# Values of two steps dealt together, three buffers of probabilities, one pair of lows less, head shares and epsilon on GpSimd

## The chip, the core and the metric

The kernel runs on one core of a Trainium2 chip, as one launch. The metric is the time of the launch on the device in microseconds, as the median of several runs. The engines are named as in the profile: PE is TensorE, with PEld its weight loads, DVE is VectorE, ACT is ScalarE, POOL is GpSimd, SP is SyncE, which here only issues DMAs.

## What is computed

Eight batches of 512 tokens with 256 features go through four blocks one after the other. They hold six attentions of 16 heads with 16 features a head: in block 0 a self-attention with a window of 64 and a linear bias and a cross-attention to the context, in block 1 a causal self-attention and a cross-attention (both with folded projections), in block 2 a cross-attention of normalized inputs, in block 3 a last cross-attention. Blocks 0 to 2 also have a feed-forward of 1024 features. The core of the reference is, for each attention:

```python
q = (qx @ wq + bq).reshape(Bq, Lq, H, DH).transpose(0, 2, 1, 3)
k = (kx @ wk + bk).reshape(Bq, Lk, H, DH).transpose(0, 2, 1, 3)
v = (kx @ wv + bv).reshape(Bq, Lk, H, DH).transpose(0, 2, 1, 3)
s = jnp.einsum('bhqd,bhkd->bhqk', q, k) / jnp.sqrt(DH)    # + bias, masked
a = jax.nn.softmax(s, axis=-1)
o = jnp.einsum('bhqk,bhkd->bhqd', a, v).transpose(0, 2, 1, 3).reshape(Bq, Lq, D)
x = _layernorm(x + o @ wo + bo, g, b)                      # then gelu(x @ w1 + b1) @ w2 + b2
```

## The kernel before

The work is 48 loops: for each pair of batches the six attentions, and within one attention the even batch and then the odd one (`LOOPS`). A loop (b, a) has 16 steps: 4 groups of 4 heads, each over 4 tiles of 128 keys. Its kinds of work, called stages, are these:

- `scores` b, a, n, e (L890, with L893 or L895 for masks): for step n, keys on the partitions and up to 512 queries in the columns, in two halves e of two heads (one half where the columns are few). They fill one of two PSUM pairs `st`. ACT takes the exponential of a pair into `probs` (L1066), which has two buffers of 4 x 512 columns.
- `values` b, a, n (L915): four heads side by side in groups of 32 columns of TensorE, probabilities in fp32 moving, accumulated over the 4 key tiles into `pv`. A step shows as 8 records of 128*32. PE waits for the exponentials of the step; the exponential of step n waits until the values of step n-2 are done.
- `sums` (L1075): ACT copies `pv` of a group into `sums`. `heads` (L1163 to L1184): DVE transposes it into `turned`, takes the reciprocal of the denominators (`rec`), multiplies (`normal`, the "shares", L1176), and for every second group transposes `normal` into `oT`.
- `low` b, "o", p: `oT` is split into a high part `oh` by ACT (L1034) and a low part `ol` by POOL (L1276). The same stages split the layer's input x into `xh`, `xl` and the context into `ch`, `cl`. They are fp32r operands of the products of L564.
- `max` (L867): for a later loop's or a later group's heads PE computes the scores once more with bf16 operands, one matmul of up to 512 columns for 128 queries, into one of three PSUM banks `mx`; DVE reduces each to the row maximum (L1149, or L1152 with a mask). POOL masks the queries for it (`qm`, L1259), up to four heads ahead (`RING`). The same three banks take the projections, the output product, and `rows` and `add`.
- `rows`, `stats`, `scale`, `turn`: output product and residual, layer norm, and the transposition back. In `stats` DVE computes mean and variance, adds epsilon (`spread_of`, L1214), and POOL raises it to the power -0.5 (`rstd`, L1287).

Every engine runs the stages in one common order, `PLAN`, each taking its own part of a stage and waiting on semaphores for the others' parts. `PLAN` is dealt from up to six streams: 0 the steps of this loop (`step_stages`), 1 the maxima of this loop, 2 "between", which is the tail of the loop before and the start of the next one, 3 the context's part of the next loop, 4 the weights, 5 the folding at the start. `MERGE` holds for each kind of loop a string of digits: the stream from which the next stage is taken. In stream 0 the values of step n-1 stand behind the scores of step n. The first `low` of an attention's output stands in stream 0 in group 2, the second in the tail.

## Time and profile before

| | us |
|---|---|
| median of 3 runs | 3447.16 |
| lowest and highest | 3444.5, 3450.5 |
| the profiled execution | 3444.64 |
| its span, first to last instruction | 3442.4 |
| PE busy | 3285.2 |
| DVE busy | 2632.1 |
| ACT busy | 2181.7 |
| POOL busy | 1701.0 |

The span is one execution of the program. A busy time is the union of an engine's instructions; matmuls overlap in the pipeline and their ends are modelled, so that short stalls of PE vanish in its busy time, and only starts tell them. The mean granted clock of TensorE is 0.994 of full speed. The chain of work that ended last is spread over many lines: 67% of the span on PE and 22% on DVE. POOL and DVE work at the same time most of the time.

### The profile page before, as it was taken

How to read it: one execution, taken by the hardware profiler on the slowest of the kernel's cores; microseconds unless marked ns; L12 is line 12 of the kernel's file. 1: busy time of each engine (PE TensorE's matmuls, PEld its weight loads, DVE VectorE, ACT ScalarE, POOL GpSimd, SP SyncE). 2: the span in 40 equal slices, each digit the busy share in tenths (PEclk: the TensorE clock that was granted, in tenths of full speed). 3: DMA queues.
4: the chain of work that ended last, by engine and by line, in shares of the span. 5: the costliest groups of instructions: out<-in, count | busy, mean ns of one | idle time of the engine just before them, and what ended most of it. 6: DMA issues, size and time to landing. Idle time of an engine off the chain costs nothing.

```text
span 3442.4 us, 57665 instructions
## 1 busy us (share of the span) xinstructions
PE 3285.2 (95%) x20149; PEld 1782.5 (52%) x20436; DVE 2632.1 (76%) x6523; ACT 2181.7 (63%) x2831; POOL 1701.0 (49%) x1497
## 2 busy tenths in 40 slices
PE   7999999999999999999999999999999999999998
PEld 5556545544555655554454565554446456455443
DVE  4976887766897697866789669776689966977667
ACT  3565766666666666666656656666575666766665
POOL 6634654444663464444475345344457435533443
PEclk9999999999999999999999999999999999999999
DMA  7322421223321232122343132122234322212211
GB/s 220 122 63 69 132 73 63 87 68 106 117 94 53 92 116 66 62 84 69 114 128 99 53 103 89 59 66 84 75 123 127 103 66 87 88 49 74 75 62 56
DMA packets 304449, 304.23 MB, mean 88 GB/s; under 512 B 52050, under 2 KB 278226, under 8 KB 302226
## 3 DMA queue, kind: packets, MB, share of 16 engines
q1 hardware_dynamic: 278436, 298.18, 27.2%
q10 hardware_dynamic: 25728, 2.36, 0.6%
q8 instruction: 165, 2.70, 0.3%
q14 instruction: 120, 0.98, 0.1%
HBM read 217.60 MB, written 82.84 MB: 87 GB/s over the span
## 4 chain that ended last, share of the span: by engine, by line
PE 67%; DVE 22%; issue 3%; ACT 3%; POOL 2%; DMA 1%; SPq 1%; POOLq 0%; another core or an unknown queue 0%; ACTq 0%; DVEq 0%
PE pv L915 12%; DVE row_max L1149 11%; PE st L890 11%; PE mx L867 10%; PE mx L564 10%; PE st L564 10%; PE mx L971 6%; PE mx L949 3%; DVE mx L1152 2%; DVE y L1220 2%; PE mx L967 2%; ACT probs L1066 2%; DVE normal L1176 1%; DVE turned L1172 1%; PE st L986 1%
## 5 line engine op out<-in xcount | busy, mean ns | idle before, releaser
L1066 ACT ACTIVATE probs<-st 128x1024 f32<-128x1024 f32 (+1 forms) x1344 | 1271.6, 976 | 693.0 <-PE st L890 435.6
L1149 DVE TENSOR_REDUCE row_max<-mx 128x1 bf16<-128x512 f32 x2048 | 1296.6, 683 | 217.2 <-PE mx L867 167.6
L1259 POOL TENSOR_TENSOR qm<-q_high,own_rows 128x512 bf16<-128x512 bf16 x768 | 794.7, 1047 | 463.1 <-PE mx L867 424.4
L867 PE MATMUL mx<-k_high,qm 128*128 128x512 bf16 (+3 forms) x2785 | 816.3, 343 | 64.0 <-DVE row_max L1152 25.0
L890 PE MATMUL st<-q_packed,k_packed 97*128 97x512 bf16 (+2 forms) x3072 | 804.8, 345 | 32.0 <-ACT probs L1066 15.1
L915 PE MATMUL pv<-probs,va 128*32 128x512 f32 (+2 forms) x6144 | 703.9, 532 | 10.7 <-ACT probs L1066 3.7
L867 PEld LDWEIGHTS mx<-k_high,qm 128*128 128x128 bf16 x3072 | 267.3, 97 | 685.4 <-DVE row_max L1149 220.6
L890 PEld LDWEIGHTS st<-q_packed,k_packed 97*128 97x128 bf16 (+1 forms) x3072 | 279.3, 98 | 357.6 <-ACT probs L1066 111.4
L1152 DVE CUSTOM_DVE_ANT_0 mx<-mx,tab 128x192 f32<-128x192 f32 (+4 forms) x1024 | 399.8, 441 | 80.4 <-PE mx L867 63.2
L1287 POOL TENSOR_TENSOR rstd<-spread_of,m_half 128x2 f32<-128x2 f32 x144 | 99.9, 694 | 484.9 <-DVE spread_of L1214 484.4
L915 PEld LDWEIGHTS pv<-probs,va 128*32 128x32 f32 x6144 | 124.9, 108 | 243.6 <-issue 196.5
L1195 DVE TENSOR_TENSOR y<-mx,row 128x256 f32<-128x256 f32 x224 | 92.5, 421 | 201.6 <-PE mx L971 173.3
L971 PE MATMUL mx<-w2s,hid 128*128 128x256 f32 x1024 | 231.6, 379 | 0.0
L1276 POOL TENSOR_TENSOR ol<-oT,oh 128x512 fp32r<-128x512 f32 x96 | 122.4, 1275 | 217.4 <-ACT oh L1034 217.4
L1276 POOL TENSOR_TENSOR xl<-xT,xh 128x512 fp32r<-128x512 f32 x116 | 148.6, 1282 | 156.9 <-ACT xh L1034 156.6
L1081 ACT ACTIVATE hid<-st,col 128x512 f32<-128x512 f32 x192 | 121.6, 685 | 130.6 <-PE st L564 130.1
L971 PEld LDWEIGHTS mx<-w2s,hid 128*128 128x128 f32 x1024 | 189.5, 190 | 23.1
L1265 POOL TENSOR_TENSOR sq<-raw_w,sq 128x512 fp32r<-128x512 f32 x93 | 119.5, 1285 | 143.0 <-ACT sq L1016 143.0
L564 PE MATMUL st<-xh,w1s 128*128 128x512 f32 x384 | 162.3, 423 | 0.0
L1075 ACT ACTIVATE sums<-pv 128x512 f32<-128x512 f32 x192 | 114.8, 598 | 67.2 <-PE pv L915 59.0
L564 PE MATMUL st<-xh,w1l 128*128 128x512 f32 x384 | 151.7, 395 | 0.0
L1220 DVE TENSOR_SCALAR y<-y,moments,rstd 128x256 f32<-128x256 f32 x288 | 145.8, 548 | 5.0 <-POOL rstd L1287 4.9
(119 smaller groups left out, 4752.9 us busy)
## 6 DMA issues: line engine op xcount, KB each, us to landing
k_packed<-k_parts_dram SPq DMA_DIRECT2D x576, 128.0 KB, 2.7
q_packed<-q_parts_dram SPq DMA_DIRECT2D x576, 128.0 KB, 2.7
q_parts_dram<-q_low SPq DMA_DIRECT2D x96, 256.0 KB, 2.1
k_parts_dram<-k_low SPq DMA_DIRECT2D x96, 256.0 KB, 2.2
raw_w<-squares_dram SPq DMA_DIRECT2D x69, 256.0 KB, 3.0
q_parts_dram<-q_high SPq DMA_DIRECT2D x48, 256.0 KB, 2.1
k_parts_dram<-k_high SPq DMA_DIRECT2D x48, 256.0 KB, 2.1
raw_w<-w_dram SPq DMA_DIRECT2D x48, 256.0 KB, 2.9
```

What stands on the lines that cost most here:

```text
L564: mm = pe.matmul(bank, stationary.bitcast(F32R), moving.bitcast(F32R), start=start and n == 0, stop=stop and n == len(parts) - 1)
L867: mm = pe.matmul(bank[:, 0:k1 - k0], qm[:, h % RING, i * P:(i + 1) * P], high["k"][s][:, t, k0:k1], start=True, stop=True)
L890: mm = pe.matmul(flat[:, c:c + w], kk[:, k * P:(k + 1) * P], qq[:, q0:q1], start=True, stop=(k_kind == FULL))
L915: mm = pe.matmul(pv[j * PAIR:(j + 1) * PAIR, q0:q1], va[s][:, k, at:at + PAIR], probs[:, step % 2, c:c + q1 - q0], start=(k == 0 and k_kin ...
L971: mm = pe.matmul(bank[:, 0:D], hid[:, j, at], w2s[:, j, :], start=False, stop=(j == FT - 1))
L1066: act.activation(dst[:, :, 0:w], held["scores", b, a, n, e][:, :, 0:w], ACT.Exp, scale=ATT_SCALE[a]) \
L1081: ins = act.activation(hid[:, n], held["hid", b, f, c][:, e], FFN_ACT[f], bias=cv(f"b1_{f}")[:, n:n + 1])
L1149: ins = dve.tensor_reduce(top, scores, AX_X, ALU.max, negate=True)
L1152: ins = dve.tensor_tensor_reduce(scores, scores, hide[:, hide.shape[1] - (k1 - k0):hide.shape[1]], -1.0, 1e30, ALU.add, ALU.min, top)
L1220: ins = dve.tensor_scalar(y[:, i, :], y[:, i, :], moments[:, i, 0:1], rstd[:, i:i + 1], ALU.subtract, ALU.mult)
L1259: pool.tensor_tensor(qm[:, h % RING], high["q"][s][:, h // HT], own_rows[:, h % HT:h % HT + 1].to_broadcast([P, TOK]), ALU.mult) \
L1276: pool.tensor_tensor(rests[:, k, at].bitcast(F32R), raw(b, tag)[:, k, at], highs[:, k, at], ALU.subtract) \
```

## The change

It does six things. (1) `step_stages` yields the values of two steps, n-2 and n-1, behind the scores of every even step n, and the last two at the end. (2) `probs` has three buffers (`RING_P`), and the exponential of step n waits for the values of step n-3. (3) `oh` and `ol` are gone: the attention output uses `xh` and `xl`, the first `low` of it moves from the steps to the tail, and attention 4's two lows follow both of its additions. `low_reads` makes ACT wait for the last reader of x before it writes them. (4) The shares are made by POOL, and DVE waits for them before it transposes `normal` into `oT` and before the next group's transpose into `turned`. (5) POOL adds epsilon before it raises to the power. (6) All strings of `MERGE` are new; they have the same digits of each kind in another order, save for the stages that moved between streams. Of the strings the diff below shows the first lines of two.

```diff
--- before.py
+++ after.py
@@ -25,6 +25,7 @@
 AHEAD = GRP + 2
 BLK = 32
 RING = 4
+RING_P = 3
 STEPS = NG * TT
 VCOL = HD + 1
 VROW = H * VCOL + HD - 1
@@ -213,12 +214,12 @@
             yield "scores", b, a, n, e
         if k == 2 and g:
             yield "heads", b, a, g - 1
-            if g == 2:
-                yield "low", b, f"o{a}", 0
-        if n:
+        if n and n % 2 == 0:
+            yield "values", b, a, n - 2
             yield "values", b, a, n - 1
             if k == 0:
                 yield "sums", b, a, g - 1
+    yield "values", b, a, STEPS - 2
     yield "values", b, a, STEPS - 1
     yield "sums", b, a, NG - 1
 
@@ -228,7 +229,10 @@
     if tag in TAG_COL:
         for t in range(KT):
             yield "add", b, tag, t
-            if tag in SPLIT_TAGS:
+            if tag in SPLIT_TAGS and tag != "a4":
+                yield "low", b, tag, t
+        if tag == "a4":
+            for t in range(KT):
                 yield "low", b, tag, t
         return
     yield "rows", b, tag, 0
@@ -251,6 +255,7 @@
 
 def tail_stages(b, a):
 
+    yield "low", b, f"o{a}", 0
     yield "heads", b, a, NG - 1
     yield "low", b, f"o{a}", 1
     for tag in AFTER[a]:
@@ -331,36 +336,36 @@
 
 
 MERGE = {
-    "first": "111111141121151101111511125011241012510111011011001515101151120001105110251000101120110112425022"
...
-    "51": "110011011201102000110413111210301112110113400111011100011011412011010030212111010121301041010140"
...
+    "first": "111115145151141145010115511511101051112120110110415101112241510011101041150514105210121012510110"
...
+    "51": "100101110110114013111400211110110110211100100200140114210131001100111421011120301310100113300012"
...
 }
 
 
@@ -404,16 +409,14 @@
         elif kind == "hidden":
             last[low_place(b, FFN_INPUT[stage[2]])] = "st", ("hid", b, *stage[2:])
         elif kind == "add" and stage[2] == "a4":
-            last["o"] = "mx", stage
+            last["x"] = "mx", stage
         elif kind == "rows" and stage[2][0] == "a":
-            last["o"] = "mx", stage
+            last["x"] = "mx", stage
     return before_low
 
 
 def low_place(b, tag):
 
-    if tag[0] == "o":
-        return "o"
     return "c" if tag[0] == "c" or tag == "in" and prefetched(b, 0) else "x"
 
 
@@ -489,13 +492,11 @@
 
         ncT = sb("ncT", [P, KT, TOK])
         oT = sb("oT", [P, KT, TOK])
-        oh = sb("oh", [P, KT, TOK])
-        ol = sb("ol", [P, KT, TOK])
         xh = sb("xh", [P, KT, TOK])
         xl = sb("xl", [P, KT, TOK])
         ch = sb("ch", [P, KT, TOK])
         cl = sb("cl", [P, KT, TOK])
-        lows = {"o": (oh, ol), "x": (xh, xl), "c": (ch, cl)}
+        lows = {"x": (xh, xl), "c": (ch, cl)}
         turned = sb("turned", [P, TOK])
         normal = sb("normal", [P, TOK])
         y = sb("y", [P, TT, D])
@@ -505,7 +506,7 @@
         in_dram = {"q": q_dram, "k": k_dram}
         qm = sb("qm", [P, RING, TOK], BF16)
         max_rows = sb("max_rows", [P, NG, BLK], BF16)
-        probs = sb("probs", [P, 2, GRP * TOK])
+        probs = sb("probs", [P, RING_P, GRP * TOK])
         sums = sb("sums", [P, 2, TOK])
         hid = sb("hid", [P, FT, TOK])
         x_next = [hid[:, s * KT:(s + 1) * KT] for s in range(SLOTS)]
@@ -913,7 +914,7 @@
                         c = column(k_kind, k, j)
                         at = place(g * GRP + j) * VCOL
                         mm = pe.matmul(pv[j * PAIR:(j + 1) * PAIR, q0:q1], va[s][:, k, at:at + PAIR],
-                                       probs[:, step % 2, c:c + q1 - q0],
+                                       probs[:, step % RING_P, c:c + q1 - q0],
                                        start=(k == 0 and k_kind != WINDOW), stop=(k == TT - 1))
                     mm.then_inc(*step_done.mark(("values", b, a, n)))
                 elif kind == "hidden":
@@ -937,7 +938,7 @@
                     bank = held["add", b, "a4", t] = mx_bank()
                     at = slice(t * P, (t + 1) * P)
                     product(pe, bank, [(weight("o", w)[:, j, at], x[:, j, :]) for j in range(KT)
-                                       for w, x in ((0, oh), (1, oh), (0, ol))], True, True) \
+                                       for w, x in ((0, xh), (1, xh), (0, xl))], True, True) \
                         .then_inc(*mx_filled.mark(("add", b, "a4", t)))
                 elif kind == "add":
                     tag, t = stage[2:]
@@ -974,7 +975,7 @@
                             pe.wait_ge(*pool_step.past(("split", b // SLOTS * SLOTS, int(tag[1]), "o")))
                             pe.wait_ge(*pool_step.past(("low", b, f"o{tag[1]}", 1)))
                         mm = product(pe, bank[:, 0:D], [(x[:, j, at], weight("o", w)[:, j, :]) for j in range(KT)
-                                                        for x, w in ((oh, 0), (oh, 1), (ol, 0))], False, True)
+                                                        for x, w in ((xh, 0), (xh, 1), (xl, 0))], False, True)
                     mm.then_inc(*mx_filled.mark(("rows", b, tag, i)))
                 elif kind == "turn":
                     tag, half = stage[2:]
@@ -1058,11 +1059,11 @@
                     q0, q1 = span(k_kind, k)
                     w = (q1 - q0) * len(heads) // 2
                     step = LOOP_NO[b, a] * STEPS + n
-                    if step >= 2:
-                        act.wait_ge(*step_done.nth(step - 1))
                     act.wait_ge(*st_filled.past(("scores", b, a, n, e)))
+                    if step >= RING_P:
+                        act.wait_ge(*step_done.nth(step - RING_P + 1))
                     c = column(k_kind, k, heads[0])
-                    dst = probs[:, step % 2, c:c + 2 * TOK].rearrange("p (b n) -> p b n", b=2)
+                    dst = probs[:, step % RING_P, c:c + 2 * TOK].rearrange("p (b n) -> p b n", b=2)
                     act.activation(dst[:, :, 0:w], held["scores", b, a, n, e][:, :, 0:w], ACT.Exp, scale=ATT_SCALE[a]) \
                         .then_inc(*st_drained.mark(("probs", b, a, n, e)))
                 elif kind == "sums":
@@ -1165,22 +1166,16 @@
                     t, odd = divmod(g, 2)
                     old = (b, a, g - 1) if g else (*before(b, a), NG - 1) if LOOP_NO[b, a] else None
                     blocks = turned[:].rearrange("p (n c) -> p n c", c=BLK)
-                    shares = normal[:].rearrange("p (n c) -> p n c", c=BLK)[:, :, odd * HD:(odd + 1) * HD]
                     dve.wait_ge(*sums_kept.past(("sums", b, a, g)))
                     if old:
-                        dve.wait_ge(*row_step.past(("shares", *old)))
+                        dve.wait_ge(*pool_step.past(("shares", *old)))
                     chain(dve.transpose(turned[:], sums[:, g % 2]), ("turned", b, a, g))
-                    chain(dve.reciprocal(rec[:], blocks[:, :, HD]), ("rec", b, a, g))
-                    if old and not odd:
-                        dve.wait_ge(*row_step.past(("oT", old[0], old[1], old[2] // 2)))
-                    share = dve.tensor_tensor(shares, blocks[:, :, 0:HD],
-                                              rec[:].unsqueeze(2).to_broadcast([P, TOK // BLK, HD]), ALU.mult)
-                    share.then_inc(*row_step.mark(("shares", b, a, g)))
+                    dve.reciprocal(rec[:], blocks[:, :, HD]).then_inc(*row_step.mark(("rec", b, a, g)))
                     if odd:
                         if LOOP_NO[b, a] and not t:
                             pb, pa = before(b, a)
                             dve.wait_ge(*mx_filled.past(("add", pb, "a4", KT - 1) if pa == 4 else ("rows", pb, f"a{pa}", TT - 1)))
-                        dve.wait_ge(*row_step.past(("shares", b, a, g)))
+                        dve.wait_ge(*pool_step.past(("shares", b, a, g)))
                         dve.transpose(oT[:, t], normal[:]).then_inc(*row_step.mark(("oT", b, a, t)))
                 elif kind == "rows":
                     tag, i = stage[2:]
@@ -1210,9 +1205,7 @@
                     chain(ins, ("stats", b, tag, half))
                     for i in (2 * half, 2 * half + 1):
                         ins = dve.bn_aggr(moments[:, i, :], st6[:, i, :])
-                    chain(ins, ("moments", b, tag, half))
-                    dve.tensor_scalar(spread_of[:, at], moments[:, at, 1], EPS, None, ALU.add) \
-                        .then_inc(*row_step.mark(("eps", b, tag, half)))
+                    ins.then_inc(*row_step.mark(("moments", b, tag, half)))
                 elif kind == "scale":
                     tag, half = stage[2:]
                     dve.wait_ge(*pool_step.past(("rstd", b, tag, half)))
@@ -1280,10 +1273,24 @@
                     pool.wait_ge(*act_step.past(("m", b, a, m)))
                     pool.tensor_tensor(low[m][:, 1], rest[m][:], low[m][:, 0], ALU.subtract) \
                         .then_inc(*pool_step.mark(("l", b, a, m)))
+                elif kind == "heads":
+                    a, g = stage[2:]
+                    t, odd = divmod(g, 2)
+                    old = (b, a, t - 1) if t else (*before(b, a), NG // 2 - 1) if LOOP_NO[b, a] else None
+                    blocks = turned[:].rearrange("p (n c) -> p n c", c=BLK)
+                    shares = normal[:].rearrange("p (n c) -> p n c", c=BLK)[:, :, odd * HD:(odd + 1) * HD]
+                    pool.wait_ge(*row_step.past(("rec", b, a, g)))
+                    if old and not odd:
+                        pool.wait_ge(*row_step.past(("oT", *old)))
+                    pool.tensor_tensor(shares, blocks[:, :, 0:HD], rec[:].unsqueeze(2).to_broadcast([P, TOK // BLK, HD]), ALU.mult) \
+                        .then_inc(*pool_step.mark(("shares", b, a, g)))
                 elif kind == "stats":
                     tag, half = stage[2:]
                     at = slice(2 * half, 2 * half + 2)
-                    pool.wait_ge(*row_step.past(("eps", b, tag, half)))
+                    pool.wait_ge(*row_step.past(("moments", b, tag, half)))
+                    pool.tensor_scalar(spread_of[:, at], moments[:, at, 1], EPS, None, ALU.add) \
+                        .then_inc(*pool_step.mark(("eps", b, tag, half)))
+                    pool.wait_ge(*pool_step.past(("eps", b, tag, half)))
                     pool.tensor_tensor(rstd[:, at], spread_of[:, at], m_half[:, at], ALU.pow) \
                         .then_inc(*pool_step.mark(("rstd", b, tag, half)))
                 elif kind == "out" and b + 1 < B:
```

## Rows read from the trace of the kernel before

**Rows 1.** The page: busy us, share of the span and instructions of each engine.

```profile
PE 3285.2 (95%) x20149; PEld 1782.5 (52%) x20436; DVE 2632.1 (76%) x6523; ACT 2181.7 (63%) x2831; POOL 1701.0 (49%) x1497
```

**Rows 2.** Busy us by stretch: sum over six DVE loops, then over six PE loops.

```profile
sum 324.40, PE 309.04 PEld 162.09 DVE 296.44 ACT 216.89 POOL 199.54; mean PE 51.51 PEld 27.01 DVE 49.41 ACT 36.15 POOL 33.26
...
sum 519.90, PE 503.36 PEld 276.85 DVE 359.71 ACT 328.43 POOL 224.19; mean PE 83.89 PEld 46.14 DVE 59.95 ACT 54.74 POOL 37.37
```

**Rows 3.** PE in order of time: start, duration, engine, line, what, count.

```profile
1510.84 0.60 PE L890 MATMUL st<-q_packed,k_packed 97*128 97x512 bf16 x2
1511.28 0.38 PE L867 MATMUL mx<-k_high,qm 128*128 128x512 bf16 x1
...
1515.86 0.59 PE L867 MATMUL mx<-k_high,qm 128*128 128x512 bf16 x2 [0.16 <-issue]
1516.39 1.06 PE L915 MATMUL pv<-probs,va 128*32 128x512 f32 x8
1517.39 0.39 PE L867 MATMUL mx<-k_high,qm 128*128 128x512 bf16 x1
```

**Rows 4.** PE in order of time: a joined pair of steps, and one step alone.

```profile
425.42 0.86 PE L915 MATMUL pv<-probs,va 128*32 128x256 f32 x16
426.21 0.61 PE L867 MATMUL mx<-k_high,qm 128*128 128x512 bf16 x2
...
405.67 0.64 PE L915 MATMUL pv<-probs,va 128*32 128x256 f32 x8
406.25 0.23 PE L867 MATMUL mx<-k_high,qm 128*128 128x128 bf16 x1
```

**Rows 5.** All engines in order of time: the last score step.

```profile
3419.18 1.04 PE L890 MATMUL st<-q_packed,k_packed 97*128 97x512 bf16 x4
...
3419.88 1.94 ACT L1066 ACTIVATE probs<-st 128x1024 f32<-128x1024 f32 x2 [0.32 <-PE st L890]
...
3421.88 1.06 PE L915 MATMUL pv<-probs,va 128*32 128x512 f32 x8 [0.66 <-ACT probs L1066]
```

**Rows 6.** Groups by line and shape: count, busy, mean ns, idle before.

```profile
L1066 ACT ACTIVATE probs<-st 128x1024 f32<-128x1024 f32 x1120 | 1107.0, 1022 | 540.1 <-PE st L890 435.6 <-PE st L893 59.1 <-DVE max_rows L1161 8.9
```

**Rows 7.** Waits: who waited for whom, us in total, times, longest.

```profile
PEld mx L867 <- POOL qm L1259: 28.6, 40, 0.8
...
ACT probs L1066 <- PE pv L915: 13.2, 10, 2.6
```

**Rows 8.** Line 1176 (ns min, median, max), and its busy time in six DVE loops.

```profile
L1176 DVE TENSOR_TENSOR normal<-turned,rec x192: 424/426/2384, 66.7 to 3424.7; 128x256 f32<-128x256 f32 x192
...
sum 324.40, DVE 17.26; mean DVE 2.88
```

**Rows 9.** Groups by line and shape, on DVE.

```profile
L1214 DVE TENSOR_SCALAR spread_of<-moments 128x2 f32<-128x2 f32 x144 | 25.4, 176 | 4.9
```

**Rows 10.** Groups by line and shape, on POOL.

```profile
L1259 POOL TENSOR_TENSOR qm<-q_high,own_rows 128x512 bf16<-128x512 bf16 x768 | 794.7, 1047 | 463.1 <-PE mx L867 424.4 <-ACT q_high L1001 19.4 <-remote 18.5
L1276 POOL TENSOR_TENSOR ol<-oT,oh 128x512 fp32r<-128x512 f32 x96 | 122.4, 1275 | 217.4 <-ACT oh L1034 217.4
...
L1287 POOL TENSOR_TENSOR rstd<-spread_of,m_half 128x2 f32<-128x2 f32 x144 | 99.9, 694 | 484.9 <-DVE spread_of L1214 484.4
```

**Rows 11.** In order of time: the last epsilon and its power.

```profile
3436.24 0.17 DVE L1214 TENSOR_SCALAR spread_of<-moments 128x2 f32<-128x2 f32 x1
...
3436.49 1.06 POOL L1287 TENSOR_TENSOR rstd<-spread_of,m_half 128x2 f32<-128x2 f32 x1 [2.66 <-DVE spread_of L1214]
```

**Rows 12.** In order of time: DVE and POOL around one multiplication of shares.

```profile
969.38 2.15 POOL L1281 TENSOR_TENSOR k_low<-k_rest,k_low 128x1024 bf16<-128x1024 f32 x1
969.42 2.38 DVE L1176 TENSOR_TENSOR normal<-turned,rec 128x256 f32<-128x256 f32 x1
```

**Rows 13.** In order of time: from the last reciprocal to the last transpose.

```profile
3424.38 0.25 DVE L1173 RECIPROCAL rec<-turned 128x16 f32<-128x16 f32 x1
...
3425.13 0.71 DVE L1184 STREAM_TRANSPOSE oT<-normal 128x512 f32<-128x512 f32 x1
```

56 lines of the change are left out of this document (28 added, 28 removed).

## The prediction

> **What bounds the kernel now.** I read the page's busy shares first, then tables by stretch, and only then single instructions. The shares say PE 95% and DVE 76% of the span [rows 1]. Both are too full for an average to tell which one sets the time where, so I cut the span at the last values step of each loop. A group of twelve loops (two batches by six attentions) takes 844 us and recurs four times; I read the second, 897.2 to 1741.5 us. Its loops fall into two classes. In six of them, 324.4 us together, DVE is busy 296.44 us, 91%; in the other six, 519.9 us, PE is busy 503.36 us, 97%, and DVE only 359.71 us, 69% [rows 2]. I call them the DVE loops (attention 0 of both batches, 1 and 3 of the even batch, 2 and 5 of the odd one) and the PE loops. A microsecond saved on PE counts in the PE loops; one saved on DVE counts in the DVE loops; ACT and GpSimd are the fullest engine in neither.
>
> Next I looked at what "busy" PE does around a values step. Eight records of 128*32 are one step. Two ordinary matmuls of 512 columns lie 0.44 us apart from start to start over the pair (1510.84 to 1511.28), 0.22 each. Two that start at 1515.86 should therefore end their streaming at 1516.30; the values step starts at 1516.39, 0.09 late, and the matmul behind it starts 1.00 after it (1517.39) [rows 3]. What part of that 1.00 belongs to entering and leaving the 32-column form is seen where two steps stand together. A pair of 256 and 128 columns takes 0.79 us to the next matmul (425.42 to 426.21); alone, 256 columns take 0.58 (405.67 to 406.25) [rows 4]. From 512 to 256 columns is 0.42 less, so 128 alone should take 0.21 less again, 0.37, and the two alone 0.95. So a step that joins another saves 0.15 or 0.16 inside and 0.09 in front: 0.24 us.
>
> **Part 1: values side by side, -31 us.** Expanding the two order lists (8566 stages each, 5895 of them with matmuls, the same work) and keeping what PE runs, the 768 values steps form 751 blocks before and 517 after. Only 251 of the 384 pairs really stand together; in the rest, most often two or three maxima stand between, so such a pair still enters and leaves twice. Blocks in the PE loops go from 380 to 252: 128 x 0.24 = 31 us. In the DVE loops they go from 371 to 265, worth 25 us if PE were the bound there; I take 0, since PE then only waits longer for a bank of maxima, and keep 25 for the range.
>
> **Part 2: score banks, +22 us.** Scores use two PSUM pairs, and a pair is refilled only after its exponential. From the start of a half's two matmuls (3419.18) it is 0.44 to the end of streaming and 0.26 more until ACT starts (3419.88, 0.32 idle before it). Two exponentials end at 3421.82 and PE follows at 3421.88 [rows 5]; one is 1.02 us [rows 6]. A bank is thus gone for 0.26 + 1.02 + 0.06 = 1.34 us after its last column. While values stand between two scores stages this is hidden by 1 us or more. In the new order a pair of values is followed by two steps of scores with only maxima between. I counted the scores whose bank was filled two stages earlier with nothing between but other scores and maxima: 96 before, 361 after. With 0.44 for the other half and 0.22 for each maximum, 1.34 falls short by 0.90, 0.68, 0.46, 0.24 and 0.02 us at 0, 1, 2, 3 and 4 maxima. Before: 4, 8, 24, 43 and 17 cases, 31 us; after: 16, 24, 61, 154 and 86 cases, 97 us. The difference, 66 us, is too much: the second half of a step mostly counts the first half's wait again (33 left), and two thirds of it, like the time, lies in the PE loops: 22 us. Bounds: 0, if other work of the merged order fills it, and 66.
>
> Three buffers of probabilities only take away a wait. ACT waited for a values step 13.2 us in all, 10 times [rows 7]; I give it nothing, because what ACT does sooner must still wait for scores.
>
> **Part 3: shares leave DVE, -27 us in the DVE loops.** Before, each of the 192 head groups has a tensor_tensor of normal on DVE, median 426 ns and longest 2384; in the six DVE loops it takes 17.26 us [rows 8], in the four groups 69 us. The epsilon addition has 144 instructions of 176 ns [rows 9]; 46 lie in the DVE loops, 8 us. Together 77 us leave DVE there. What comes back: for odd groups DVE issues rec and then waits for the shares, since the transpose into oT needs them, and everything behind it on DVE, the maxima above all, waits too. GpSimd takes 1275 ns for 128x512 [rows 10], so half of it, 0.64, for 128x256 is my estimate (bounds: 0.42, DVE's own, and 1.28, the whole row). A hop to GpSimd costs 0.08 (3436.24 + 0.17 to 3436.49) [rows 11]; I take 0.10 for the one back, so 0.82 if GpSimd is free. In these loops it is busy 199.54 of 324.4 us [rows 2], 62%, so sometimes a mask of 1.05 us [rows 10] is still running; I take 0.23 for that, 1.05 in all. 48 odd groups x 1.05 = 50 us. 77 - 50 = 27 us. Even groups wait for nothing on DVE until the next group, four steps later. In the PE loops both changes are covered by DVE's 31% idle time; without that cover they would cost 0.4 us for each odd group, 19 us, less the even ones' gain.
>
> GpSimd gets 192 x 0.64 and 144 epsilons. Its smallest tensor_tensor, rstd, is 694 ns [rows 10], so I price epsilon between 0.17 and 0.69; at the upper end that is 123 + 99 us on an engine that is 49% busy [rows 1]. Being in order it also holds the masks of later heads behind rec. It already idles 484.4 us before its 144 powers until the epsilon is there [rows 10], while PE's weight loads wait for masks 28.6 us in all [rows 7]; four masks of lead cover it, and I give it 0.
>
> The same rows hold a fact on the port. At 969.42 DVE's shares take 2.38 us, and end 0.27 us after the GpSimd subtraction that had begun at 969.38 [rows 12]. The Trainium skill, SBUF — State Buffer, section Who interferes with whom, says that a DVE instruction with two SBUF inputs and a GpSimd one that reads SBUF exclude each other for the whole instruction, and Perfetto Trace Analysis, section Optimizing Scalar/DVE Operations, warns that moving work between the two might therefore not help. The trace agrees with the lock. By it, what the 24 shares of the six DVE loops take beyond their median, 17.26 - 24 x 0.426 = 7 us a group, 28 us in all, goes away with the instruction, while DVE's remaining instructions of that kind meet a GpSimd that is busy somewhat longer. By the warning part 3 would be 0 and the time 27 us higher; the row speaks for the gain, because maxima read PSUM and one input.
>
> **Part 4: one pair of lows less, +2 us.** The attention output's high and low now use those of x, written only after x's last reader. In the order lists every reader of xh (project, project_v, hidden, the output product) stands earlier in the same stream "between", so ACT finds that wait over; behind it stand exponentials, which would be what waits. The first half, which was made at step 10, is now made at the start of the next loop's tail: 96 lows, 1.28 on GpSimd [rows 10] and, as estimate, half of that on ACT, as before, only later, under the next loop's steps. Attention 4's two lows follow both additions now; eight times, hidden by other streams. Only the last tail is bare. There rec ends at 3424.63 and oT starts at 3425.13 [rows 13]. The moved low starts when the last sums end, about 1.0 us before rec does, and takes 0.63 + 0.07 + 1.28 by the durations above, so it holds GpSimd until 3425.6; the shares then end at 3426.2, and oT starts 1.2 us late. Epsilon before the last rstd adds up to 0.5. I take 2, bounds 1 and 3.
>
> **Sum.** -31 + 22 - 27 + 2 = -34. The profiled execution took 3444.64 us, with a span of 3442.4; 3410.6 by that. The median of the three runs, 3447.16, is 2.5 above it, so I predict 3413 us.
>
> **The rivals.**
> A, all of it pays: part 1 in all loops (-56), no new waits at the banks (0), odd groups at 0.82 (77 - 39 = -38). -94 + 2 = -92, 3355 by the median. For it: the new order gives values more lead behind their scores, and the third buffer lets ACT run on. Against: the bank counts, and DVE at 91%. Its likelier part is the stretch between 3355 and 3387.
> B, the change doesn't do what it says: the joined steps are separated anyway by a wait for the second step's probabilities, so part 1 is 0, and the rest, +22 - 27 + 2 = -3, leaves 3444. For it: where the last two steps stood together in full attention, the second left PE idle for 0.66 us until ACT had finished [rows 5]. Against: the lead of values behind scores grows in the new order.
> C, slower: DVE held by GpSimd. If an odd group finds a k_low of 2.15 us [rows 12] in front of its shares, DVE waits 3.0. It decides from 77 / 48 = 1.6 us: beyond that the shares cost more than they free. At 2.5: 48 x 2.5 - 77 = +43; -31 + 22 + 43 + 2 = +36, 3483. For it: GpSimd at 62% and in order. Against: GpSimd idled 484.4 us for its epsilons [rows 10], so it mostly gets there first.
> D, slower: the bank waits whole (+66), with parts 1 and 3 as forecast and DVE's gain halved because PE no longer feeds it: -31 + 66 - 13 + 2 = +24, 3471.
>
> **How the numbers follow.** My forecast (3387 to 3437) has 0.40, A 0.18, B 0.15, C 0.13, D 0.14. Differences under 0.2%, 7 us, are about what a measurement of this kernel can't tell from none. Faster: forecast and A, 0.58. Same: B, 0.15. Slower: C and D, 0.27. The range leaves out half of A's far end and the upper parts of C and D: 3365 to 3475; the forecast's own is 3387 to 3437.
>
> **What the profile after would show.** Part 1: 517 blocks of values, a weight load of values preceded by idle "issue" less often, and the DVE loops hardly shorter on PE's account. Part 2: more PE idle time before scores, ended by ACT's probabilities. Part 3: no shares on DVE, 192 new ones on GpSimd near 0.64 us, DVE busy about 2485 us, and idle before oT's transpose about 1.05 us, 96 times. Part 4: the last stretch from the final sums to the end 2 us longer. The prediction is wrong if the PE loops get longer (then D), if DVE's idle time before oT is above 1.6 us (C), or if the DVE loops shrink by more than 4% (A).

## The result, and the profile after

The changed kernel takes 3438.49 us in the median of 8 runs (3433.87 to 3443.64), the kernel before 3447.14 in 8; the ratio is 0.9977, with a 95% interval of 0.9968 to 0.9986. That is 8.7 us less where 34 were forecast. The profiled execution took 3439.88 us, with a span of 3438.0.

First the page: its head, the chain of work that ended last, and three groups (busy, mean ns | idle before, releaser).

```profile
span 3438.0 us, 57661 instructions
...
PE 3271.4 (95%) x20153; PEld 1806.6 (53%) x20436; DVE 2488.6 (72%) x6187; ACT 2169.4 (63%) x2823; POOL 1845.0 (54%) x1833
...
PE 68%; DVE 16%; POOL 6%; ACT 4%; issue 3%; DMA 1%; SPq 1%; POOLq 0%; ACTq 0%; another core or an unknown queue 0%; DVEq 0%
...
L1252 POOL TENSOR_TENSOR qm<-q_high,own_rows 128x512 bf16<-128x512 bf16 x768 | 792.6, 1042 | 345.0 <-PE mx L868 277.1
...
L1291 POOL TENSOR_SCALAR spread_of<-moments 128x2 f32<-128x2 f32 x144 | 31.7, 220 | 430.6 <-DVE moments L1207 430.6
...
L1285 POOL TENSOR_TENSOR normal<-turned,rec 128x256 f32<-128x256 f32 x192 | 119.5, 622 | 207.6 <-DVE rec L1173 181.2
```

Set beside [rows 1], DVE lost 143.5 us and PE 13.8. The chain shows the same: DVE holds 16% of it instead of 22%. The span fell by 4.4 us only. Second, the stretches: the same twelve loops, cut at their last values steps (892.9 to 1736.2 us), first the six DVE loops, then the six PE loops.

```profile
sum 324.80, PE 307.19 PEld 166.42 DVE 277.32 ACT 216.34 POOL 216.66; mean PE 51.20 PEld 27.74 DVE 46.22 ACT 36.06 POOL 36.11
...
sum 518.50, PE 502.09 PEld 279.36 DVE 341.45 ACT 325.96 POOL 243.06; mean PE 83.68 PEld 46.56 DVE 56.91 ACT 54.33 POOL 40.51
```

Against [rows 2] DVE has 19 us less to do in the DVE loops of this group, and they take 0.4 us more (324.80 for 324.40); the PE loops take 1.4 less. Third, the waits (us in total, times, longest).

```profile
POOL normal L1285 <- DVE rec L1173: 181.2, 106, 5.4
PEld mx L868 <- DVE row_max L1150: 178.2, 352, 0.8
...
PEld st L891 <- ACT probs L1067: 142.8, 272, 1.2
...
ACT sums L1076 <- PE pv L916: 105.3, 116, 1.9
...
DVE oT L1179 <- POOL normal L1285: 82.4, 92, 2.1
...
PEld mx L868 <- POOL qm L1252: 48.7, 77, 0.8
...
ACT probs L1067 <- PE pv L916: 14.8, 12, 2.2
```

The same waits in the kernel before; those for `qm` and of `probs` for values were 28.6 and 13.2 us [rows 7]:

```profile
PEld mx L867 <- DVE row_max L1149: 220.6, 375, 1.4
...
PEld st L890 <- ACT probs L1066: 111.4, 201, 1.2
...
ACT sums L1075 <- PE pv L915: 59.0, 52, 2.4
```

By these rows PE waits less for maxima's banks, more for score banks, and ACT stands longer in front of the copy of `sums`, which now follows a joined pair.

These waits overlap with other instructions. A sum comes from the starts of all matmuls. What lies between two starts beyond the streaming of the first (the shortest distance at which the trace shows that form, 0.22 us for 512 columns of scores or maxima) is put down to the matmul that came late. For a block of values, 0.09 us in front of it and 0.15 inside are taken off as its switch, and gaps of less than 0.02 us are left out. In some traces up to 287 of the 3072 matmuls of the maxima have no record; such a matmul is taken to start with its weight load, but not before the one in front of it has streamed. "Scores" below is such lateness in front of matmuls into `st`, "maxima" in front of all into `mx`, in us over the span.

| kernel | blocks of values | late scores | late maxima | late values | median us |
|---|---|---|---|---|---|
| before | 751 | 91 | 200 | 28 | 3447.1 |
| after | 517 | 140 | 206 | 19 | 3438.5 |

Switching saves (751 - 517) x 0.24 = 56 us; 49 come back in front of scores and 6 in front of maxima; 9 fewer are lost in front of values. -56 + 49 + 6 - 9 = -10, and the spans differ by 4.4. Such sums meet the measured differences below to within some 7 us, no better. The same cut by loops shows where even that lies: the first loop takes 94.4 us instead of 100.4, and all others with the tail together 1.6 more.

### The profile page after: what moved, and what is told of

It reads as the page before. It is cut to its first block, busy times and chain, and to the rows that moved or that the text cites. A ratio compares the mean times of both kernels' runs of the same rounds, so it can differ in the third digit from the quotient of the medians.

```text
span 3438.0 us, 57661 instructions
## 1 busy us (share of the span) xinstructions
PE 3271.4 (95%) x20153; PEld 1806.6 (53%) x20436; DVE 2488.6 (72%) x6187; ACT 2169.4 (63%) x2823; POOL 1845.0 (54%) x1833
## 4 chain that ended last, share of the span: by engine, by line
PE 68%; DVE 16%; POOL 6%; ACT 4%; issue 3%; DMA 1%; SPq 1%; POOLq 0%; ACTq 0%; another core or an unknown queue 0%; DVEq 0%
PE pv L916 13%; PE st L891 11%; PE st L565 10%; PE mx L868 10%; PE mx L565 10%; DVE row_max L1150 7%; PE mx L972 6%; PE mx L950 3%; ACT probs L1067 3%; DVE mx L1153 2%; DVE y L1213 2%; PE mx L968 2%; POOL qm L1252 1%; PE st L987 1%; DVE st L1204 1%
## 5 line engine op out<-in xcount | busy, mean ns | idle before, releaser
L1067 ACT ACTIVATE probs<-st 128x1024 f32<-128x1024 f32 (+1 forms) x1344 | 1257.3, 977 | 587.6 <-PE st L891 305.6
L868 PE MATMUL mx<-k_high,qm 128*128 128x512 bf16 (+4 forms) x2789 | 821.5, 343 | 57.4 <-DVE row_max L1153 21.2
L891 PE MATMUL st<-q_packed,k_packed 97*128 97x512 bf16 (+2 forms) x3072 | 815.7, 345 | 53.3 <-ACT probs L1067 25.9
L916 PE MATMUL pv<-probs,va 128*32 128x512 f32 (+2 forms) x6144 | 654.6, 527 | 6.0 <-ACT probs L1067 3.5
L891 PEld LDWEIGHTS st<-q_packed,k_packed 97*128 97x128 bf16 (+1 forms) x3072 | 271.3, 98 | 352.4 <-ACT probs L1067 142.8
L916 PEld LDWEIGHTS pv<-probs,va 128*32 128x32 f32 x6144 | 148.6, 109 | 281.4 <-issue 215.4
L1291 POOL TENSOR_SCALAR spread_of<-moments 128x2 f32<-128x2 f32 x144 | 31.7, 220 | 430.6 <-DVE moments L1207 430.6
L1285 POOL TENSOR_TENSOR normal<-turned,rec 128x256 f32<-128x256 f32 x192 | 119.5, 622 | 207.6 <-DVE rec L1173 181.2
L1076 ACT ACTIVATE sums<-pv 128x512 f32<-128x512 f32 x192 | 114.1, 594 | 122.1 <-PE pv L916 105.3
L1269 POOL TENSOR_TENSOR xl<-oT,xh 128x512 fp32r<-128x512 f32 x96 | 122.0, 1271 | 94.1 <-ACT xh L1035 94.1
L565 PE MATMUL mx<-xh,sq 128*128 128x512 f32 x480 | 143.7, 416 | 13.5 <-POOL sq L1258 12.3
```

Of the source, the lines that this page charges most:

```text
L565: mm = pe.matmul(bank, stationary.bitcast(F32R), moving.bitcast(F32R), start=start and n == 0, stop=stop and n == len(parts) - 1)
L868: mm = pe.matmul(bank[:, 0:k1 - k0], qm[:, h % RING, i * P:(i + 1) * P], high["k"][s][:, t, k0:k1], start=True, stop=True)
L891: mm = pe.matmul(flat[:, c:c + w], kk[:, k * P:(k + 1) * P], qq[:, q0:q1], start=True, stop=(k_kind == FULL))
L916: mm = pe.matmul(pv[j * PAIR:(j + 1) * PAIR, q0:q1], va[s][:, k, at:at + PAIR], probs[:, step % RING_P, c:c + q1 - q0], start=(k == 0 and ...
L1067: act.activation(dst[:, :, 0:w], held["scores", b, a, n, e][:, :, 0:w], ACT.Exp, scale=ATT_SCALE[a]) \
L1269: pool.tensor_tensor(rests[:, k, at].bitcast(F32R), raw(b, tag)[:, k, at], highs[:, k, at], ALU.subtract) \
```

## The experiments

All ratios are to the kernel before on the same chip, with 95% intervals. The median of before lay between 3446.0 and 3447.1 us. Some expectations give lateness at other levels than the table (for before and after 97 and 152 us of late scores, or 131 for after, where the table has 91 and 140) and 238 blocks less for 234; the measured texts all go by the table's count.

### What the moved shares are worth in the new order (e1, e7)

A function in the kernel chooses where the shares of even (0) and odd (1) groups are computed; on DVE they stand behind `rec` as in the kernel before.

```diff
+def ON_DVE(odd):
+    return odd in (0, 1)          # e1; e7: odd in (1,)
...
+                    if ON_DVE(odd):
+                        dve.wait_ge(*row_step.past(("rec", b, a, g)))
+                        dve.tensor_tensor(shares, blocks[:, :, 0:HD], ...)
...
-                elif kind == "heads":
+                elif kind == "heads" and not ON_DVE(stage[3] % 2):
```

> The changed kernel with the shares of all head groups back on DVE (everything else as changed). In the two traces the time between the kernels splits into 238 blocks of values less (-56 us), waits of PE before scores +55 us, waits of PE before maxima and other users of those three banks +6 us. Theory 1 (the waits before the maxima's banks come from how the maxima are bunched in the order, so relieving DVE's total bought little): 0 to +10 us against the changed kernel, 3438 to 3448. The forecast's own step (77 us off DVE, 50 us of waiting back): +20 to +27 us, 3459 to 3465. Rival (the wait of DVE for GpSimd in odd groups is what ate the gain): faster than the changed kernel, 3420 to 3434, and PE's waits before the maxima's banks fall.

Measured: 3473.61 us, 1.0077 (1.0064 to 1.0089). Moving the shares is worth 35 us in the new order, so the missing gain isn't missing there. The rest of the change alone, new order and joined values included, is 27 us slower than before: late scores 138, late maxima 239, so the sum gives -56 + 47 + 39 - 9 = +21. None of the three forecasts for e1 had 3474. Cut by loops, the moved shares gain 16 us in the DVE loops and 16 in the PE loops.

> The changed kernel with the shares of odd groups on DVE and those of even groups on GpSimd. DVE idles 85.6 us before oT's transposes in the changed kernel; with odd shares on DVE that becomes 96 x 0.43 to 0.64, 41 to 61 us of work, and no wait. By that alone 0 to 15 us below the changed kernel. All shares on DVE cost 35 us; if that is per instruction (0.18 us each), this one is 17 us above the changed kernel. Theory 2 has no word on the sign.

Measured: 3436.48 us, 0.997 (0.996 to 0.9979), the same as after within its interval. In the new order DVE's wait for odd shares costs what its own odd shares would; the even ones make the gain.

### The old order with the other parts (e2, e5), and shares alone in the kernel before (e6, f1)

e2 is the changed code with the stages and strings of before: values of step n-1 behind the scores of step n. Only the first `low` stands elsewhere than before, directly before the heads of group 3. e5 is e2 with all shares on DVE. e6 and f1 are the kernel before with nothing but shares moved: all of them, and even ones alone.

> The changed kernel with the old order of stages: values of step n-1 behind the scores of n, the old merge strings, only the first low of the attention output moved to just before the last head group (it has to be, since it shares x's buffers). So it has the three buffers, the one pair of lows less, and shares and epsilon on GpSimd, but no joined values: 751 blocks. Theory 1: parts 2 to 4 alone are worth little, 3437 to 3450. The forecast (part 3 worth 27 us in any order): 3415 to 3425. Rival (GpSimd's part costs): 3455 or more.

Measured: 3606.67 us, 1.0461 (1.0446 to 1.0475).

> The changed kernel with the old order of stages and the shares on DVE: of the change it keeps three buffers, the one pair of lows less with the first low moved to the tail, and epsilon on GpSimd. The same with shares on GpSimd took 3606.7 us; there DVE waited 199.9 us before 92 of its transposes into oT, 2.2 us each, against 0.9 in the changed kernel. Theory 3 (in the old order the shares stand behind other GpSimd work, here the moved low of 1.28 us and what waits for it, and every group holds DVE): 80 to 130 us less, 3475 to 3525; the rest is the moved low's. Rival (the shared lows alone cost the 160 us): 3590 or more.

Measured: 3457.94 us, 1.0033 (1.0022 to 1.0043). So in the old order three buffers, the lows of x and epsilon together cost 11 us, and the shares cost 149. e5 and e1 differ in nothing but the order: late scores 92 and 138, late maxima 204 and 239, 234 blocks fewer, so -56 + 46 + 35 - 9 = +16, and e1 is 16 us slower. With the shares on DVE the new order loses.

> The kernel before with only the shares moved to GpSimd (part 3 alone without epsilon; order, lows and buffers as before). If DVE's wait in odd groups is near 0.9 us as in the changed kernel: 20 to 35 us below before, 3412 to 3427. Theory 3 (the wait depends on what stands before the shares in GpSimd's order, which the old order was not made for): DVE waits 1.5 us and more, 3445 to 3500.

Measured: 3520.98 us, 1.0214 (1.0194 to 1.0234), 74 us more than before, from the one move that is worth 35 us in the new order. The waits before the transpose into `oT` (us, times, longest), first of e6, then of e2:

```profile
DVE oT L1178 <- POOL normal L1286: 133.7, 92, 5.1
```

```profile
DVE oT L1182 <- POOL normal L1288: 199.9, 92, 5.2
```

That is 1.45 and 2.17 us each, with the longest at 5.2, against 82.4 / 92 = 0.90 in after. The longest kind is seen in e2, all engines in order of time:

```profile
1803.25 3.04 POOL L1255 TENSOR_TENSOR qm<-q_high,own_rows 128x512 bf16<-128x512 bf16 x3
...
1806.00 0.25 DVE L1176 RECIPROCAL rec<-turned 128x16 f32<-128x16 f32 x1
...
1806.24 2.14 POOL L1277 TENSOR_TENSOR q_low<-q_rest,q_low 128x1024 bf16<-128x1024 f32 x1
...
1808.34 2.12 POOL L1277 TENSOR_TENSOR k_low<-k_rest,k_low 128x1024 bf16<-128x1024 f32 x1
...
1810.42 0.62 POOL L1288 TENSOR_TENSOR normal<-turned,rec 128x256 f32<-128x256 f32 x1
...
1811.14 0.71 DVE L1182 STREAM_TRANSPOSE oT<-normal 128x512 f32<-128x512 f32 x1 [4.89 <-POOL normal L1288]
...
1812.15 0.34 PE L871 MATMUL mx<-k_high,qm 128*128 128x192 bf16 x1 [4.11 <-DVE row_max L1156]
```

`rec` is there at 1806.25, but POOL, in order, has the next loop's `q_low` and `k_low` first; DVE stands for 4.89 us, and PE behind it for 4.11, because nobody empties its banks of maxima.

> The kernel before with the shares of even groups on GpSimd and those of odd groups on DVE; nothing else changed. All shares on GpSimd cost 74 us in this order, with DVE idle 133.7 us before 92 transposes into oT. Theory 4 (what costs is DVE waiting for GpSimd in odd groups, by how much stands before the shares in GpSimd's order): the 74 us go away and 96 x 0.64 = 61 us less on DVE help a little: 0 to 20 us below before, 3427 to 3447. Rival (GpSimd itself is short of time, or its masks come late): 3460 or more.

Measured: 3443.25 us, 0.9994 (0.9985 to 1.0003). With odd shares back on DVE the 74 us are gone. The cost is DVE's wait for odd shares and what follows from it, not POOL's work. And the even shares, worth 37 us in the new order (e1 to e7), are worth nothing that these runs can tell in the old one.

What follows from the wait is not only idle time. The mean granted clock is 0.983 in e6 and 0.994 in before; if the missing share is time at half clock, e6 has 120 us of it and before 41. As an estimate, half of the difference, at most 39 of the 74 us, is slower streaming behind the long waits (the last section shows one). How much of the 74 is the clock and how much the waits is not settled more closely.

### What a joined pair costs and saves (e8, e4, e3, f2)

e8 takes the joined pairs of after apart: the first step of a pair that stood together moves in front of the stage with matmuls before it, and nothing else changes. All 768 steps then stand alone.

> The changed kernel with each of its 251 joined pairs separated: the first of the two values steps is moved up before the one matmul stage in front of it. 768 blocks instead of 517, all else in place. If a joined pair saves 0.24 us wherever it stands: +60 us, 3490 to 3500. If half of it is hidden because DVE or ACT is the bound there: +25 to +35. Rival (joining is worth nothing): within 10 us of the changed kernel.

Measured: 3504.37 us, 1.0166 (1.0147 to 1.0185), 66 us more than after. 251 more blocks x 0.24 = 60 us; late scores are 144 and late maxima 206, together 4 more, and late values 25, 6 more. The price of a switch holds, and in all loops: the DVE loops have 119 blocks more and take 28 us more, the PE loops 132 and 40. But the banks' lateness doesn't fall when the pairs are taken apart with one stage in between: it belongs to the new order as a whole, not to the joined blocks alone.

e4 goes the other way: in after, every even step's values move directly before the odd step's, so that all 384 pairs stand together. e3 is the same edit on e2, and f2 on e5.

```diff
+for n, stage in enumerate(PLAN):
+    if stage[0] == "values" and stage[3] % 2:
+        m = PLAN.index(("values", *stage[1:3], stage[3] - 1))
+        PLAN.insert(n - 1, PLAN.pop(m))
```

> The changed kernel with all 384 pairs joined: where maxima or other work stood between the two values steps of a pair, the first is moved down to the second. 384 blocks instead of 517, the cases of early refilled score banks unchanged (337). Theory 1: 133 x 0.24 = 32 us less, of which some comes back as waits for the maxima's banks: 3408 to 3425. Rival (part 1 pays only where PE is the bound, 54% of the separated pairs): 3421 to 3428. Rival (joining doesn't pay): 3438 or more.

Measured: 3493.31 us, 1.0135 (1.0121 to 1.0148), 55 us slower than after. Switching falls by (517 - 384) x 0.24 = 32 us, but late scores rise from 140 to 155 and late maxima from 206 to 279, 88 together.

> As the one before, but every even step's values are put directly before the odd step's: 384 blocks instead of 751, nothing else moved. Theory 1: 367 x 0.24 = 88 us of switching gone, against score banks refilled without values between (338 cases instead of 76, as many as in the changed kernel): +50 to +60 us; so 25 to 40 us below the kernel before it, near 3405 to 3425. Rival (joined steps wait for the second step's probabilities anyway, so that joining is worth nothing): no faster than the kernel before it.

Measured: 3740.78 us, 1.085 (1.0835 to 1.0865), 134 us slower than e2.

> Old order on the changed kernel's buffers with shares on DVE (3457.9 us), with every pair of values joined: 384 blocks instead of 751. Where the shares were on GpSimd, joining cost 134 us: 88 us of switching gone, waits at the score banks +90 and at the maxima's banks +144. Theory 4 (the joined block itself starves both sets of banks; an order not made for it pays more than it saves): 40 to 110 us above 3457.9, so 3500 to 3570. Rival (it was only the wait for GpSimd that joining made worse): 3380 to 3430.

Measured: 3614.24 us, 1.0486 (1.0471 to 1.05), 156 us slower than e5. Late scores go from 92 to 186, late maxima from 204 to 365: -88 for switches, +255 for banks, -10 for values, 157 by that sum. So it isn't DVE's wait for shares that makes joining dear in the old order. Its two largest waits behind banks, of f2:

```profile
PEld mx L880 <- DVE row_max L1162: 232.4, 486, 1.8
...
PEld st L903 <- ACT probs L1079: 169.4, 253, 1.3
```

Here the joined blocks themselves starve the banks, in an order that wasn't made for them. What happens at a joined pair is seen in after, in order of time:

```profile
1508.15 1.02 ACT L1067 ACTIVATE probs<-st 128x1024 f32<-128x1024 f32 x1 [0.22 <-PE st L891]
...
1508.60 0.38 PE L868 MATMUL mx<-k_high,qm 128*128 128x512 bf16 x1
...
1508.91 1.92 PE L916 MATMUL pv<-probs,va 128*32 128x512 f32 x16
...
1509.86 0.65 DVE L1150 TENSOR_REDUCE row_max<-mx 128x1 bf16<-128x512 f32 x1
...
1510.43 0.70 DVE L1172 STREAM_TRANSPOSE turned<-sums 128x512 f32<-128x512 f32 x1
...
1510.60 1.02 ACT L1067 ACTIVATE probs<-st 128x1024 f32<-128x1024 f32 x1 [1.42 <-PE pv L916]
1510.77 0.10 PEld L868 LDWEIGHTS mx<-k_high,qm 128*128 128x128 bf16 x1 [0.84 <-DVE row_max L1150]
```

For 1.86 us (1508.91 to 1510.77) PE fills no bank of scores or maxima. ACT stands 1.42 us of it, released by the values: in this row the exponential itself waits for its buffer, which it does only 12 times in the span; mostly ACT stands before `sums` instead. DVE empties one bank, and at 1510.43 goes on to the heads' transpose. So from 1510.77 PE has scores and maxima to fill at once, a maximum in 0.22 us and a half of scores in 0.44, which the others empty in 0.65 and 1.02.

### Is it the length of the exponentials or of the maxima? (h1 to h4)

h1 (kernel before) and h2 (after) take the exponentials of half the columns from the seventh loop on. h3 and h4 take the unmasked maxima over half the columns from there on.

```diff
+                    part = w if LOOP_NO[b, a] < 6 else w // 2                               # h1, h2
-                    act.activation(dst[:, :, 0:w], held[...][:, :, 0:w], ...)
+                    act.activation(dst[:, :, 0:part], held[...][:, :, 0:part], ...)
...
+                    part = (k1 - k0) // (1 if LOOP_NO[b, a] < 6 or k_kind != FULL else 2)   # h3, h4
-                    scores, top = held["max", b, a, h, i][:, 0:k1 - k0], ...
+                    scores, top = held["max", b, a, h, i][:, 0:part], ...
```

> The kernel before with every exponential from the seventh loop on over half its columns (so the other half of the probabilities is left as it was; this work is left out). A score bank is then free about 0.5 us sooner. PE's waits before scores in the trace of before are 97 us by start times. Theory 2 (the changed order trades 56 us of switching for 55 us more of score-bank waits and some 35 us more of waits at the maxima's banks, of which the shares on GpSimd take 35 us back): 60 to 90 us below the kernel before, 3357 to 3387.

> The changed kernel with the same exponentials halved. PE's waits before scores are 152 us in the changed kernel's trace. Theory 2: the 55 us between the two go away, so this one is 45 to 65 us below the other halved kernel. Rival (the give-back is not in the score banks): it stays 5 to 20 us below, as with whole exponentials.

Measured: h1 3454.08 us, 1.0022 (1.0012 to 1.0031); h2 3439.97, 0.9983 (0.9974 to 0.9992). The exponentials of h1 by the page:

```profile
L1067 ACT ACTIVATE probs<-st 128x512 f32<-128x512 f32 (+3 forms) x1344 | 800.1, 612 | 944.2 <-PE st L890 627.1
```

ACT loses 471 us of work (800.1 for 1271.6), and the kernel gets no faster. Late scores fall from 91 to 78, late maxima rise from 200 to 220; in h2 from 140 to 110, and from 206 to 240. A bank of scores that is free sooner is paid for at a bank of maxima.

> The kernel before with every row maximum of the full attentions from the seventh loop on taken over half its columns (683 down to about 420 ns; this work is left out), and the exponentials' scale made tiny there so that they stay finite, which changes no duration. PE's waits before users of the maxima's banks are 209 us in before. Theory 2: 80 to 150 us below the kernel before.

> The changed kernel with the same maxima halved. Theory 2: with DVE's total out of the way in the loops with full attention, the score-bank waits (+55 us) stay and the switching gain (56 us) stays, and part 3's relief of DVE is worth less: between 10 us above and 15 us below the other kernel with halved maxima. Rival (the maxima's banks are what ate the gain): 30 to 55 us below it.

Measured: h3 3416.01 us, 0.9907 (0.9892 to 0.9922); h4 3421.56, 0.9925 (0.991 to 0.994). Late maxima fall from 200 to 155 and from 206 to 174, late scores rise from 91 to 100 and from 140 to 154. Shorter maxima gain 31 us before and 17 after, out of 473 us that these instructions lose in h3 (823.6 for 1296.6):

```profile
L1150 DVE TENSOR_REDUCE row_max<-mx 128x1 bf16<-128x256 f32 (+1 forms) x2048 | 823.6, 437 | 546.9 <-PE mx L867 534.3
```

So most of the lateness in front of maxima isn't their length. What is left is that DVE is at something else in its queue or that maxima come in bursts; no run here parts these two.

### Is it the copy of the sums? (g1, g2)

ACT's wait before `sums` had grown by 46 us (105.3 against 59.0) and is in front of the next exponentials. g1 is after with these copies of groups 0 to 2 moved behind the scores of the next group's second step; g2 does it in m1 (below), in the kinds that keep the new order.

```diff
+for b, a in LOOPS:
+    for g in range(NG - 1):
+        n = PLAN.index(("sums", b, a, g))
+        last = max(m for m, stage in enumerate(PLAN) if stage[:4] == ("scores", b, a, TT * g + TT + 1))
+        if last > n:
+            PLAN.insert(last, PLAN.pop(n))
```

> The changed kernel with one stage moved: the copy of the value sums of groups 0 to 2 stands behind the scores of the next step instead of right behind the joined pair of values, 144 of 192 copies. ACT is in order, and in the changed kernel it stood idle before these copies until PE had finished the values for 105.3 us, 116 times, against 59.0 us and 52 times in the kernel before. Theory (the copy behind a joined pair is what keeps the score banks full): the next exponentials start up to 0.9 us sooner, ACT's wait for values falls below 60 us, PE's wait before scores falls from 131 to about 105 us, and the time falls by 10 to 25 us, 3413 to 3428. Rival (the bank waits come from the pair itself, during which PE feeds nobody, and from what stands queued behind it): ACT's wait falls as well, but PE's waits before scores and maxima together stay within 10 us of 284 and the time within 7 us of 3438.

> The mixed orders (shares of even groups on GpSimd, of odd ones on DVE, four kinds of loops in the old order), which took 3430, with the copies of the sums moved as in the run before in the kinds that keep the new order. By the first theory two thirds of its gain comes on top, 3413 to 3423. By the rival nothing changes: 3427 to 3433.

Measured: g1 3450.34 us, 1.001 (1.0001 to 1.0019), 12 slower than after; g2 3434.72, 0.9967 (0.9954 to 0.9979), 5 slower than m1. The 5 of g2 are within the intervals, the 12 of g1 are not. ACT's wait is shorter, as foretold, but PE's waits for score banks are what they were, 142.8 us in after (of g1):

```profile
PEld st L897 <- ACT probs L1073: 143.4, 268, 1.2
...
ACT sums L1082 <- PE pv L922: 51.7, 46, 1.7
...
PE pv L922 <- ACT sums L1082: 4.1, 8, 0.6
...
PE pv L918 <- ACT sums L1082: 3.8, 6, 0.8
```

Late scores are 141 for 140 and late maxima 204 for 206. So the first theory falls: the copy doesn't hold the score banks. The rival is right on the banks and wrong on the time, because the moved copy has a price of its own. There is only one `pv`, so the next group's first values wait for its copy; these waits are the last two rows, after has none of them, and late values rise from 19 to 29, 10 of the 12 us.

### Orders mixed by kind of loop (m1, m2)

Cut by loop, after is slower than before by over 2 us in three kinds: attention 0 of the odd batch (49.5 us for 47.1), and 2 (80.2 for 77.7) and 4 (94.2 for 91.6) of the even one. In attention 1 of the odd batch e5, in the old order, is shorter than e7 (86.2 for 87.1). m1 keeps odd shares on DVE as e7, and gives these four kinds the stages and strings of before (the first `low` stays in the tail).

```diff
+OLD_KINDS = ((0, 1), (1, 1), (2, 0), (4, 0))
-    steps, maxima = list(step_stages(b, a)), ...
+    steps, maxima = list((old_step_stages if (a, b % SLOTS) in OLD_KINDS else step_stages)(b, a)), ...
-        for turn in MERGE[key]:
+        for turn in (OLD_MERGE if (a, b % SLOTS) in OLD_KINDS else MERGE)[key]:
```

> The changed kernel with odd shares on DVE (3436.5 us), and in four of twelve kinds of loops (attention 0 odd, 1 odd, 2 even, 4 even) the old order and its merge strings, in which values follow one by one. By the loops' mean times in the traces of this kernel and of the old order on the same buffers with shares on DVE, these kinds take 2.8, 0.9, 0.4 and 1.4 us less in the old order, 5.5 us a group and 22 in all: 3414 to 3422. Rival (a loop's time depends on what order the loops around it have, or even shares on GpSimd cost in the old order): 3430 or more.

Measured: 3430.06 us, 0.9959 (0.9946 to 0.9973), the lowest median of the complete kernels here, 16 less than that of before beside it (14 by the ratio) and 8 less than after. It is faster than before; against after and e7 the intervals overlap, so the gain from mixing is likely and not shown. Blocks 593, late scores 115, late maxima 195. Against e7, attention 4 of the even batch gained 2.0 us a loop (91.9 for 93.9), but the loop behind it, attention 4 of the odd one, gave back 3.8 (87.0 for 83.2), though its own order is that of e7: a loop's time depends on the order of the loop before it.

> As the mixed orders, but with all shares on DVE in the four kinds of loops that have the old order. If even shares on GpSimd are harmless in the old order: the same within 5 us; if the old order can't take them: 5 to 20 us less than the mixed orders with them, 3414 to 3420.

Measured: m2, with all shares on DVE in these four kinds, 3435.64 us, 0.997 (0.9959 to 0.9982). That is 6 us above m1 with overlapping intervals, and f1 was level with before: in the old order it isn't shown that even shares do better on GpSimd.

Two buffers of probabilities with the new order weren't tried. Read from the order of stages they can't work: in places the values of step n-2 stand behind another refill of the score banks, and that refill waits for exponentials that wait for those values. The third buffer is a condition of this order.

## Why the prediction was partly right and where it failed

**What bounds the kernel, and part 1 (forecast -31, by the blocks -56).** The price of a switch was right: e8 gives 66 us for 251 blocks. The blocks are the 517 of the forecast. Wrong was to count the PE loops alone: e8 pays in both classes of loops (DVE loops +28, PE loops +40 by the cut), so "PE only waits longer for a bank" didn't hold at 91% of DVE. The 25 us kept for the range belonged in the sum.

**Part 2 (forecast +22): this step failed.** The count of early refills gave 66 us as an upper bound, and I cut it to a third. (Counted strictly from the order lists the refills are 76 and 336 for 96 and 361, and the difference is again 67 us.) Late scores rose by 49 (26 to 52 in the DVE loops, 65 to 88 in the PE loops), 47 in e1. And a second price wasn't in the sum at all: the banks of maxima. e1 shows it bare, 200 to 239, +39, and 35 of these are the order's alone (e5 to e1). Together 86 us where 22 stood. That maxima wait because nobody fills their banks during a joined pair and they come in a burst behind it is what the rows show at one pair, and e4 and f2 add such waits by joining; how much of after's lateness is this isn't measured, since e8 leaves it in place. Rival D had the 66, but not the maxima. What the count also missed is that the waits aren't separate costs: h1 and h2 took 13 and 30 us from late scores and found 20 and 33 more in front of maxima, and h3 and h4 moved some the other way. PE alternates between two kinds of banks, and what is gained at one is met at the other.

**Part 2, the third buffer (0).** ACT's wait for values is 14.8 us for 13.2 [rows 7], so it buys no time by itself; it is what allows the joined order. e5 puts it, the lows of x and epsilon together at +11 us in the old order; no run parts them.

**Part 3 (forecast -27; its shares measured -35 in the new order).** e1 moves only the shares. Without epsilon's 8 us the forecast for them was 69 - 50 = -19, all of it in the DVE loops. Measured are -16 there and -16 in the PE loops, where DVE's idle time was said to cover them: the step "in the PE loops both changes are covered" was wrong too, in the other direction. The sizes held: a share is 622 ns for an estimate of 640, DVE is busy 2488.6 us for 2485, the wait before `oT` is (82.4 + 3.2) / 96 = 0.89 us for 1.05 (the 3.2 are waits that others end), and epsilon is 220 ns, near its lower bound [rows 9]. Weight loads wait 48.7 us for masks instead of 28.6, where I had put nothing; but they wait 42.6 in e1 too, so most of that came with the order. The gain falls mostly on late maxima (239 to 206 from e1 to after). What the text didn't see is how far it hangs on the order: e6 loses 74 us by the same move. Rival C named the mechanism, a `k_low` in front of the shares. Its threshold of 1.6 us stood for the DVE loops, and was too generous: in e6 the mean wait in these loops is just 1.60 us, and they take 52 us more, the PE loops (1.27) 27 more. A mean doesn't tell of the waits of up to 5 us, behind which PE stands too and its clock falls. The shares on GpSimd vary by 58 ns (613 to 671), those on DVE by 1960 [rows 8]. The Trainium skill, Perfetto Trace Analysis, section Optimizing Scalar/DVE Operations, warns that moving work between the two engines might not help. e6 comes out so and after doesn't; the page's reason is the shared port, while e6 loses by what stands in front of the shares in the queue.

**Part 4 (forecast +2).** The mechanism is there to the step, in after:

```profile
3419.16 1.26 POOL L1269 TENSOR_TENSOR xl<-oT,xh 128x512 fp32r<-128x512 f32 x1 [4.63 <-ACT xh L1035]
3419.35 0.25 DVE L1173 RECIPROCAL rec<-turned 128x16 f32<-128x16 f32 x1
3420.39 0.62 POOL L1285 TENSOR_TENSOR normal<-turned,rec 128x256 f32<-128x256 f32 x1
3421.04 0.71 DVE L1179 STREAM_TRANSPOSE oT<-normal 128x512 f32<-128x512 f32 x1 [1.44 <-POOL normal L1285]
```

`oT` starts 1.44 us behind `rec`, before it was 0.50 [rows 13], so 0.94 late where 1.2 was forecast; the stretch from the last values is 0.7 us longer, not 2. What the shared lows cost elsewhere no run shows by itself.

**The sum.** Forecast -31 + 22 - 27 + 2 = -34. By the runs -56 + 47 + 39 - 9 = +21 without the moved shares, where e1 measured +27, so 6 us of that are in none of these terms; and 27 - 35 = -8 with them. From -34 to -8: banks +64, switches -25, values -9, part 3 -8, tail -2, unexplained +6. The sign was right only because part 3 outweighs what the new order costs, and that part 3 did so in the PE loops was luck. None of the forecast's own signs of being wrong came up: the PE loops didn't get longer (1.2 us less in all), the wait before `oT` stayed under 1.6 us, the DVE loops didn't shrink by 4% (3.8 us of 1344). **B**'s time, 3444, was nearer than mine, but for another reason: the joined steps do stand together and do save.

## What to carry to other kernels

A longer block on the engine that feeds everybody saves its switches and starves the others; price both, for every kind of bank that it fills, and sum the waits from start times, because a wait shortened at one bank comes back at the next. Before moving an operation to an in-order engine, list what stands in front of it there in every kind of loop: the same 192 multiplications were worth -35 us and +74 us. And look at an order loop by loop: a mixture of both has the lowest median here, though its lead over after is within the intervals.
